# A four-layer state-space and attention kernel: side work laid out anew on the engines of its state-space layers

## The reference

```python
h = _layernorm(x, gamma, beta)
h = h * (1.0 + scale[:, None, :]) + shift[:, None, :]
h = h[:, perm]
xz = h @ W_in
xm, z = jnp.split(xz, 2, axis=-1)
xc = conv_general_dilated(xc, conv_w, ...) + conv_b      # four taps over time, per channel
xm = silu(xc)
dtr, Bm, Cm = split(xm @ W_xp, [64, 80])
dt = softplus(dtr @ W_dt + b_dt)
A = -exp(A_log)
def step(hst, inp):
    dA = exp(dt_t[:, :, None] * A)
    hst = hst * dA + (dt_t * x_t)[:, :, None] * B_t[:, None, :]
    y = einsum('bds,bs->bd', hst, C_t)
y = (y + xm * D_param) * silu(z)
return x + gate * (y @ W_out)[:, inv_perm]
```

## Time and profile before

| what | value |
|---|---|
| median of 3 runs | 2964.96 us (2961.61 to 2968.52) |
| the profiled execution | 2969.68 us, of which the span is 2968.0 us |
| TensorE busy | 2442.6 us, 82% of the span |
| VectorE | 2178.1 us, 73% |
| ScalarE | 2159.3 us, 73% |
| GpSimd | 1689.8 us, 57% |

### The profile page before, as it was taken

How to read it: one execution, slowest core, us unless ns; L and a number is a source line. 1 busy time by engine, 2 the same in 40 slices (tenths; PEclk the granted TensorE clock), 3 DMA queues, 4 the chain that set the end, 5 groups by cost and what they waited for, 6 DMA issues and landing times. The chain is left out here.

```text
span 2968.0 us, 44243 instructions
## 1 busy us (share of the span) xinstructions
PE 2442.6 (82%) x14532; PEld 1664.9 (56%) x14532; DVE 2178.1 (73%) x2878; ACT 2159.3 (73%) x3593; POOL 1689.8 (57%) x1365
## 2 busy tenths in 40 slices
PE   7778578898898898637888999857888888889885
PEld 4555257777677777512333333224576666677784
DVE  4443378888888898556777776615899988998983
ACT  3333389999999999513666656547989989999993
POOL 0000078888988989650111111004989889899895
PEclk9999799999999999867999999878999999999997
DMA  3100211112112111145555544111111112112121
GB/s 106 39 28 22 73 40 45 51 60 65 39 60 67 37 53 60 38 93 81 80 87 87 82 82 76 22 55 43 44 67 60 58 53 78 61 53 74 58 68 43
DMA packets 106124, 177.01 MB, mean 60 GB/s; under 512 B 10709, under 2 KB 91405, under 8 KB 97199
## 3 DMA queue, kind: packets, MB, share of 16 engines
q1 hardware_dynamic: 101679, 161.69, 21.3%
q0 software_dynamic: 4224, 12.59, 1.3%
HBM read 139.70 MB, written 34.14 MB: 59 GB/s over the span
## 5 line engine op out<-in xcount | busy, mean ns | idle before, releaser
L1121 POOL TENSOR_TENSOR l_h<-l_h,l_c_all 128x512 f32<-128x512 f32 x1024 | 1380.7, 1370 | 184.8 <-DVE l_h L1038 168.9
L1038 DVE TENSOR_TENSOR_SCAN l_h<-l_dA,l_ps_dbu 128x512 f32<-128x512 f32 x1024 | 1218.8, 1209 | 205.5 <-PE l_ps_dbu L1300 102.1
L1300 PE MATMUL l_ps_dbu<-ident,l_dub 128*128 128x128 f32 x4096 | 628.1, 276 | 151.0 <-DVE l_h L1038 79.7
L909 ACT ACTIVATE l_dA<-l_dt,l_a_neg 128x512 f32<-128x512 f32 x1024 | 731.1, 715 | 7.0 <-issue 5.2
L891 ACT ACTIVATE l_dub<-l_duT,l_b_tok 128x512 f32<-128x512 f32 x1024 | 730.4, 714 | 2.4 <-PE l_ps_dbu L1300 2.0
L1285 PE MATMUL l_ps_y<-ident,l_h 128*128 128x128 f32 x4096 | 623.3, 275 | 11.8 <-POOL l_h L1121 8.8
L1300 PEld LDWEIGHTS l_ps_dbu<-ident,l_dub 128*128 128x128 f32 x4096 | 471.0, 141 | 205.0 <-DVE l_h L1038 112.0
L1285 PEld LDWEIGHTS l_ps_y<-ident,l_h 128*128 128x128 f32 x4096 | 485.5, 142 | 130.8 <-issue 92.4
L1795 ACT ACTIVATE l_probs<-l_ring 128x512 f32<-128x512 f32 x512 | 292.8, 598 | 261.9 <-PE l_ring L1933 260.7
L1614 DVE TENSOR_REDUCE l_q_max<-l_ring 128x1 f32<-128x512 f32 x512 | 338.4, 683 | 175.6 <-PE l_ring L1926 171.8
L1933 PE MATMUL l_ring<-l_qs,l_ks 102*128 102x512 bf16 x512 | 201.5, 398 | 59.5 <-DMA l_qs<-l_m_parts 51.4
(11 more groups left out here) (248 smaller groups left out, 2949.7 us busy)
## 6 DMA issues: line engine op xcount, KB each, us to landing
l_c_all<-c_rows_dram SPq DMA_DIRECT2D x64, 1024.0 KB, 4.8
l_res<-x_dram SPq DMA_DIRECT2D x24, 512.0 KB, 6.0
parts_dram<-l_parts SPq DMA_DIRECT2D x48, 256.0 KB, 2.9
l_qs<-parts_dram SPq DMA_DIRECT2D x48, 256.0 KB
l_ks<-parts_dram SPq DMA_DIRECT2D x48, 256.0 KB
l_x_in<-x_dram SPq DMA_DIRECT2D x16, 512.0 KB, 7.3
x_dram<-l_res SPq DMA_DIRECT2D x16, 512.0 KB, 3.1
l_x_in<-in_x SPq DMA_DIRECT2D x8, 512.0 KB, 4.3
```

The source lines that it names most:

```text
L909: act.activation(dA[:, s % DA_RING, :], dt[:, p, j, :], ACT.Exp, scale=a_neg[:, j * N + n:j * N + n + 1]).then_inc(da_ok, 1)
L1038: dve.tensor_tensor_scan(h[:, h_slot(s), :], dA[:, s % DA_RING, :], ps_dbu[:, dbu_slot(s), :], 0.0, ALU.mult, ALU.add).then_inc(scan_ok, 1)
L1121: pool.tensor_tensor(h[:, h_slot(s), :], h[:, h_slot(s), :], c_all[:, (n // C_GROUP) % 2, n % C_GROUP, :], ALU.mult).then_inc(hc_ok, 1)
L1300: last = pe.transpose(ps_dbu[:, dbu_slot(s), t * P:(t + 1) * P], dub[:, DUB_SLOTS[n], t, j * P:(j + 1) * P], ident[:])
```

## The change

The arithmetic of the taps and of softplus is divided anew, and most step numbers move:

- **Convolution.** The last tap and the bias become an Identity pass on ScalarE that reads the projection in PSUM, in `x_part`, ahead of its copy. VectorE keeps three taps for each block, at steps 9 to 20.
- **z copies** go from ScalarE to VectorE (`z_copy`, steps 45, 47, 49, 51, the first batch excepted).
- **Softplus** drops the absolute value: VectorE writes dt and, capped at 20, a second copy (`dt_low`); ScalarE takes exp and ln of that, and the sum becomes a maximum. Sums stand at 41, 43, 45, 47, GpSimd's `dt_u` at 42, 44, 46, 48.
- **Single contractions**: `in_proj` and `out_proj` issue a half at a step (`X_AT`, `OUT_AT`).
- **Statistics** of the normalisation go from steps 25 to 27 to 31 to 33, its ScalarE parts from 31, 36, 37 to 36, 47, 48, and `mod` from 53, 55 to 54, 56.
- **Gathers** of layer 3 go from steps 4 to 12 to 18 to 24, and from 40 to 43 to 51 to 54.
- **Edge pieces.** The first batch's Silu and x projection are cut by channel block and interleaved with its z projection.
- **Layer 2.** The three DMAs of a group's maxima are issued by GpSimd right after it has made them.
- **Semaphores** are cleared by ranges.

```diff
-                for s in self.all:
-                    sp.sem_clear(s)
+                nums = sorted(s.num for s in self.all)
+                at = 0
+                while at < len(nums):
+                    end = at + 1
+                    while end < len(nums) and nums[end] == nums[end - 1] + 1:
+                        end += 1
+                    sp.sem_clear(range(nums[at], nums[end - 1] + 1))
+                    at = end
...
-PREP_V = JB * (TAPS - 1)
+X_AT = (0, 1, 3, 4, 5, 6, 7, 8)
+OUT_AT = (20, 21, 22, 23, 25, 26, 27, 28)
+PREP_V = JB * (TAPS - 2)
...
                 def x_part(b, j):
                     act.wait_ge(in_mm, b * JB + j + 1)
+                    if j == 0 and not first(b):
+                        act.wait_ge(dt_ok, b * JB)
+                    wcol = VEC_LAYOUT[L + "_conv_w"][0] + j * TAPS + TAPS - 1
+                    act.activation(work[:, j, :], bank(b, "x", j), ACT.Identity, scale=vecs[:, wcol:wcol + 1],
+                                   bias=vec(vecs, L + "_conv_b")[:, j:j + 1])
                     act.activation(conv_in[:, j, TAPS - 1:], bank(b, "x", j), ACT.Copy).then_inc(xc_ok, 1)
-                def z_part(b, p, t):
-                    act.wait_ge(z_mm, b * TB + t + 1)
-                    if t == 0:
-                        if not early(b):
-                            act.wait_ge(y_ok, b * JB - JB)
-                    act.activation(z[:, p, t, :], bank(b, "z", t), ACT.Copy).then_inc(z_ok, 1)
+                def z_first(t):
+                    act.wait_ge(z_mm, t + 1)
+                    act.activation(z[:, 0, t, :], bank(0, "z", t), ACT.Copy).then_inc(z_ok, 1)
...
+                def silu_first(j):
+                    act.wait_ge(conv_ok, j + 1)
+                    act.activation(u[:, j, :], work[:, j, :], ACT.Silu).then_inc(u_part if j < JB - 1 else u_ok, 1)
...
-                def softplus_abs(b, j):
-                    act.wait_ge(dtr_ok, b * JB + j + 1)
-                    act.activation(work[:, j, :], dt_in[:, j, :], ACT.Abs).then_inc(dti_ok, 1)
-
                 def softplus_exp(b, j):
                     act.wait_ge(dti_ok, b * JB + j + 1)
-                    act.activation(work[:, j, :], work[:, j, :], ACT.Exp, scale=-1.0).then_inc(dt_exp, 1)
+                    act.activation(work[:, j, :], work[:, j, :], ACT.Exp).then_inc(dt_exp, 1)
...
-                    if s in (3, 6, 9, 12): x_part(b, (s - 3) // 3)
-                    if s == 33: xd(b, p)
-                    if s in (40, 42, 44, 46): softplus_abs(b, (s - 40) // 2)
-                    if s in (41, 43, 45, 47): softplus_exp(b, (s - 41) // 2)
-                    if s in (42, 44, 46, 48): softplus_log(b, (s - 42) // 2)
+                    if s in (4, 7, 9, 11): x_part(b, (4, 7, 9, 11).index(s))
+                    if s == 34: xd(b, p)
+                    if s in (39, 41, 43, 45): softplus_exp(b, (s - 39) // 2)
+                    if s in (40, 42, 44, 46): softplus_log(b, (s - 40) // 2)
                     if first(b):
-                        if s in (13, 14, 15, 16): z_part(b, p, s - 13)
-                    elif s in (45, 47, 49, 51): z_part(b, p, (s - 45) // 2)
+                        if s in (13, 16, 19, 22):
+                            silu_first((s - 13) // 3)
+                            z_first((s - 13) // 3)
+                            if s == 22:
+                                act.preload_act_table_set(EXP_LN)
                     if s in (57, 59, 61, 63): du_tok(b, (s - 57) // 2)
                 def far_step(s, b):
-                    if s == 31: ln_rstd(b)
-                    if s in (36, 37): ln_apply(b, s - 36)
-                    if s in (53, 55): mod(b, (s - 53) // 2)
+                    if s == 36: ln_rstd(b)
+                    if s in (47, 48): ln_apply(b, s - 47)
+                    if s in (54, 56): mod(b, (s - 54) // 2)
...
-                        if j == 0 and not first(b):
-                            dve.wait_ge(dt_ok, b * JB)
-                        dve.tensor_scalar(work[:, j, :], conv_in[:, j, 0:T], vecs[:, wcol:wcol + 1],
-                                          vec(vecs, L + "_conv_b")[:, j:j + 1], ALU.mult, ALU.add).then_inc(prep_v, 1)
                     else:
-                        dve.wait_ge(prep_v, b * PREP_V + j * (TAPS - 1) + k)
-                        dve.scalar_tensor_tensor(work[:, j, :], conv_in[:, j, k:k + T], vecs[:, wcol + k:wcol + k + 1], work[:, j, :],
-                                                 ALU.mult, ALU.add).then_inc(prep_v if k < TAPS - 1 else conv_ok, 1)
+                        dve.wait_ge(prep_v, b * PREP_V + j * (TAPS - 2) + k)
+                    dve.scalar_tensor_tensor(work[:, j, :], conv_in[:, j, k:k + T], vecs[:, wcol + k:wcol + k + 1], work[:, j, :],
+                                             ALU.mult, ALU.add).then_inc(prep_v if k < TAPS - 2 else conv_ok, 1)
+
+                def z_copy(b, p, t):
+                    dve.wait_ge(z_mm, b * TB + t + 1)
+                    if t == 0 and not early(b):
+                        dve.wait_ge(y_ok, b * JB - JB)
+                    dve.tensor_copy(z[:, p, t, :], misc[:]).then_inc(z_ok, 1)
+                def dt_low(b, j):
+                    dve.tensor_scalar(work[:, j, :], bank(b, "dt", j), vec(vecs, L + "_dt_b")[:, j:j + 1], SOFT_TOP, ALU.add, ALU.min).then_inc(dti_ok, 1)
...
-                    dve.scalar_tensor_tensor(dt[:, p, j, :], dt_in[:, j, :], 0.0, work[:, j, :], ALU.max, ALU.add).then_inc(dt_ok, 1)
+                    dve.scalar_tensor_tensor(dt[:, p, j, :], dt_in[:, j, :], 0.0, work[:, j, :], ALU.add, ALU.max).then_inc(dt_ok, 1)
...
-                    if 9 <= s < 9 + JB * TAPS: tap(b, (s - 9) // TAPS, (s - 9) % TAPS)
-                    if s == 34: b_copy(b, p)
-                    if s in (36, 38, 40, 42): dt_raw(b, (s - 36) // 2)
-                    if s in (43, 45, 47, 49): softplus_sum(b, p, (s - 43) // 2)
+                    if 9 <= s < 9 + JB * (TAPS - 1): tap(b, (s - 9) // (TAPS - 1), (s - 9) % (TAPS - 1))
+                    if s == 35: b_copy(b, p)
+                    if s in (36, 38, 40, 42):
+                        dt_raw(b, (s - 36) // 2)
+                        dt_low(b, (s - 36) // 2)
+                    if s in (41, 43, 45, 47): softplus_sum(b, p, (s - 41) // 2)
+                    if not first(b) and s in (45, 47, 49, 51): z_copy(b, p, (s - 45) // 2)
                 def far_step(s, b):
-                    if s in (25, 26): ln_stats(b, s - 25)
-                    if s == 27: ln_moments(b)
+                    if s in (31, 32): ln_stats(b, s - 31)
+                    if s == 33: ln_moments(b)
                 def post_step(s, b, p):
-                    if s in (24, 28): out_gate(b, p, (s - 24) // 4)
+                    if s in (24, 29): out_gate(b, p, (s - 24) // 5)
...
-                            if s == 4: next_rows(b + 2)
-                            if s in (6, 8, 10, 12): gather_x(b + 2, (s - 6) // 2)
+                            if s == 18: next_rows(b + 2)
+                            if s in (21, 22, 23, 24): gather_x(b + 2, s - 21)
                         if gathered and has_post:
-                            if s in (40, 41, 42, 43): gather_y(b - 1, 1 - p, s - 40)
-                            if s in (53, 58): residual_rows(b - 1, (s - 53) // 5)
+                            if s in (51, 52, 53, 54): gather_y(b - 1, 1 - p, s - 51)
+                            if s in (59, 62): residual_rows(b - 1, (s - 59) // 3)
...
-                        if has_prep and s in (43, 45, 47, 49): dt_u(b + 1, 1 - p, (s - 43) // 2)
+                        if has_prep and s in (42, 44, 46, 48): dt_u(b + 1, 1 - p, (s - 42) // 2)
...
+                def in_proj(b, e, k):
+                    if k:
+                        pass
+                    elif e == 0:
                         pe.wait_ge(mod_ok, b * DH + DH)
                     elif not first(b):
                         pe.wait_ge(xc_ok, b * JB + e)
-                    for k in range(DH):
-                        last = pe.matmul(bank(b, "x", e), w_in[:, k, e * P:(e + 1) * P], modT[:, k, :], start=(k == 0), stop=(k == DH - 1))
-                    last.then_inc(in_mm, 1)
+                    last = pe.matmul(bank(b, "x", e), w_in[:, k, e * P:(e + 1) * P], modT[:, k, :], start=(k == 0), stop=(k == DH - 1))
+                    if k == DH - 1:
+                        last.then_inc(in_mm, 1)
                 def z_proj(b, t):
                     if first(b):
-                        pass
+                        if t == TB - 1:
+                            pe.wait_ge(z_ok, 1)
                     elif t == 0:
-                        pe.wait_ge(dtr_ok, b * JB + JB)
+                        pe.wait_ge(dti_ok, b * JB + JB)
...
+                def x_first(k):
+                    if k < JB - 1:
+                        pe.wait_ge(u_part, k + 1)
+                    else:
+                        pe.wait_ge(u_ok, 1)
```

(26 more changed lines are left out.)

52 lines of the change are left out of this document (21 added, 31 removed).

## The result

The changed kernel takes 3018.15 us (median of 4 runs, 3016.15 to 3021.37) against 2966.74 us: a ratio of 1.0177, 95% interval 1.0158 to 1.0195. The forecast was slower, by 16 us to 2981 (2925 to 3025 as range); it is slower by 51. The direction was right and the size was not, and the parts show that one of the sum's terms did not exist and that one cost was put at nothing.

A forecast was written before the change was run, and what follows sets the result against it. ScalarE nearly bounds the steady batch; TensorE's DMA waits bound the attention layer. Layer 1 +33, layer 3 +12, softplus stall +35, layer 2 -40, clears -14, openings -10 sum to +16: 2981 us, range 2925 to 3025.

The forecast's parts named there:

- wait at step 3: Batch start: TensorE waits 3.8 us for ScalarE's conv copy, done at 6.5 us; scan 9 at 20.0 us against 14.38.
- the z loop: Batch end: z projection, transposes, scan and VectorE's z copy chain at 4.75 us per two steps; ScalarE alone 3.5.
- the stall: Softplus sum at step 45, layers 1 and 3: VectorE waits on GpSimd, 2.5 us per batch, +35 in all.
- the ring of eight: First half of a batch: ScalarE's lead of up to eight units absorbs start delay; Silu ends only 1.2 us later.
- statistics that moved behind it: Normalisation statistics after the Silu, two pairs of 0.64 us on VectorE: hidden by ScalarE's table loads, no cost.
- -40 forecast: Layer 2: maxima pass the stack on GpSimd's queue, 4.1 us per wait plus some 2 of half-clock work won.
- 3.6 us that I kept as a rest: Layer 2: of TensorE's 7.7 us wait per batch, 3.6 remain because the stack lands about 1470, TensorE ready at 1466.4.
- Clears and openings: Outside the steady batches: 246 semaphore clears become a handful, -14; earlier first x projection in each layer's opening, -10.
- 1 (the stall is short): Rival, chance 0.28: VectorE waits half a GpSimd instruction, 0.64 us, at the softplus sum; 9 instead of 35, 2955 us.
- 2 (ScalarE stays the bound): Rival, chance 0.10: VectorE copies z while TensorE works on units between; batches take 105 us, kernel 2834.
- 3 (clock): Rival, chance 0.10: TensorE runs at 0.50 clock behind the batch-start wait, 2.2 us more per batch, +31, 3012 us.
- 4 (layer 2 does not do what it says): Rival, chance 0.10: maxima on the other queue still land with the stack; -40 becomes 0, kernel 3021 us.

The follow-up runs named there:

- x_start_old: The changed kernel with whole x projections and ScalarE's conv copies at their old steps, last tap still on ScalarE: 2969.74 us.
- z_and_x: The changed kernel with z copies back on ScalarE and whole x projections and conv copies at their old steps: 2904.69 us.
- gathers_40: The changed kernel with layer 3's gathers of y and row residuals back at steps 40 to 43, 53, 58: 3066.97 us.
- half_stack: The changed kernel with half the heads left out of every layer 2 stack transfer from the third batch on: 3015.47 us.
- best1: The kernel before plus range clears, layer 3's gathers at new steps and layer 2's maxima on GpSimd's queue: 2944.07 us against 2964.01.
- z_x_tap: z_and_x with the fourth tap and bias back on VectorE (16 taps, ScalarE copies only): 2964.47 us.
- z_on_act: The changed kernel with the four z copies of a steady batch back on ScalarE at the same steps: 2970.58 us.
- l2_alone: The kernel before with only layer 2's maxima issued by GpSimd, SyncE starting the stack without them: 2964.46 us against 2969.97.

## Why the prediction was wrong

- **The two loops: right in kind.** The wait at step 3 for ScalarE's copy, which is done 6.5 us into the batch as worked out, the z loop of 4.75 us per two steps (14.85 worked out, 14.9 measured) and ScalarE's 6.8 us before the modulation copy (7.05) all are in the trace, and undoing either end of the batch gives 48 us.
- **The direction was right in part by luck.** Without the stall, which does not exist, the same sum gives 2946 us: faster than before. What made the kernel slower all the same are costs of the batch that the sum had too small or not at all. The fourteen batch periods average 116.0 us where 113.0 was worked out, which is 41 us; with the edges the scans of layers 1 and 3 grew by 84 us instead of 45.
- **The start was mis-sized.** The step "the ring of eight absorbs the rest, and the Silu at step 28 ends 1.2 us later than before" failed: the Silu of u ends at 49.1 us instead of 47.1, 2.0 later. Scan 9 comes at 21.3 and not 20.0, with the clock down behind the wait, which I had put into a rival at 0.10; the wait of 3.8 us was itself 2.16. The comparison with the kernel before also hides most of what the start costs: scan 29 is at 51.1 us before, at 53.9 in the changed kernel and at 49.1 with the old start and twelve taps (x_start_old). The start costs 4.8 us, and the taps give 2.0 of them back.
- **A wait was put at nothing.** The step "the statistics that moved behind it ... are on VectorE and hidden there by ScalarE's table loads" failed, or the move of `b_copy`, which the sum doesn't have, takes its place: TensorE waits 1.85 us for that copy, and steps 29 to 36 take 1.9 us longer in the batch worked out, 24.5 us in all fourteen. So the first z copy ends at 84.9 us and not at 82.5; from there to the next batch the forecast had 31.4 us and the trace 31.6. No run tells the statistics from the copy's new step, and z_and_x still has 23.3 us of these waits.
- **The stall of +35 does not exist.** The step that took the middle between 0.09 and 4.78 for a sum with three GpSimd instructions near it failed. The largest of the four sums of a steady batch is 0.79 us, and gathers_40 shows what it takes: GpSimd behind by several instructions. I had named the backlog and then left it out. This error and the two above cancel, which is why layers 1 and 3 came out within 5 us (84 against 80).
- **Layer 2 was the costly miss**: -40 forecast, about -8 measured in the scores. Three steps of that term failed. The wait does not end with the queue order: the maxima land when the stack's traffic ends, whichever queue issues them (12 us on GpSimd's). The part won per wait was 2.3 us, not 4.1. And the clock is not won back, since 3.83 us of idle remain by ScalarE's Silu and tables, whatever the DMAs do; in half_stack the granted clock falls to 0.50 behind them too. The 3.6 us that I kept as a rest was near that number, but for another reason.
- **Clears and openings** were forecast at -24; the stretches outside scans and scores became 30 us shorter, about 6 more than forecast. In best1, which has the clears and not the new openings, they became 15.6 shorter: the clears were sized right, and the openings somewhat low.
- Of the rivals, the condition of 1 (the stall is short) came true, but not its 2955, since it kept my prices for the loops. 2 (ScalarE stays the bound) is out for this change, and z_x_tap speaks against it even for z_and_x. 3 (clock) is partly true: 1.3 us later at scan 9, and 0.7 us per batch in the mean at steps 36 to 40; its sign, a clock of 0.9 or less in layer 1, did not come (0.97). 4 (layer 2 does not do what it says) is four fifths true.
- The sum, put right on the profile: 2986, less the stall's 35, plus 39 for the batches and 32 for layer 2, less 6 for clears and openings, is 3016, the profiled execution (3016.28).

On the rule about the shared port pair, an exclusive lock for one whole instruction (the Trainium skill, SBUF - State Buffer, section SBUF: two separate sides): in the steady batches the trace agrees, no sum waits more than one instruction. In gathers_40 sums of 2.9 and 4.2 us last over more than one GpSimd instruction, as the 5.51 did; there the measurement decides, and the rule is too short. On the rule that each DMA engine takes turns between the queues, a packet at a time (the Trainium skill, DMA: Bandwidth & Descriptors, section Queues, rings and completion order): the quick passing that I had read into it is not in the trace. Issued while the DMA engines were full, a 4 KB transfer on another queue took 12 us, until they fell idle; in half_stack, issued when they were nearly idle, it took 1.6.

Why z_and_x wins more than its two parts can be read from the traces for the most part. Against the kernel before in the same runs the changed kernel is 51 us slower, z_on_act and x_start_old lie 51 and 52 below that, and z_and_x 111: 8 more than the sum, not 17. The fourteen batch periods of the profiled executions say the same (49, 55 and 112 us). The difference comes from steps 36 to 40, which vary from batch to batch with the clock: over fourteen batches they take 111.8 us in the changed kernel, 120.5 in z_on_act, 114.3 in x_start_old and 111.3 in z_and_x. Outside them the parts add up to 115 and both together win 111. What stays open is why the clock falls there in some batches and not in others.

## What to carry to other kernels

Before a wait is priced as removable, look at what each engine does under it: the next releaser (here ScalarE's Silu passes and table loads) can stand within a microsecond of the first, and then the order of queues hardly matters. Where two engines hand one bank to and fro, put the copy on the engine that runs ahead of the chain, not on the one that stands in it, even when the other is less busy. And when two new costs are estimated, check each against the trace by its place: a sum that comes out right can hide errors that cancel.

## What the hardware showed that I had not expected

- The granted clock of TensorE was low behind short waits. Behind the 2.16 us at a batch's start it is 0.57 over the next 4 us. In z_on_act, behind 1.85 us of waiting for b_tok, it is at its lower level (0.51, 1.2 GHz) for ten microseconds of full work, and steps 36 to 40 take 11.0 us instead of 7.3. TensorE's row and the stretch behind it:

```profile
892.00 1.83 PE L1260 MATMUL l_misc<-l_x_dbl,l_w_dt 64*128 64x512 f32 x2 [1.85 <-DVE l_b_tok L1010]
...
892.00:902.00 10.00, 10.00 (x33) 6.69 (x34) 6.96 (x8) 6.79 (x12) 7.52 (x7) 0.51 0.00 0
```

- It is not so in each batch: in the changed kernel steps 36 to 40 of layer 1 take 7.3 us in five of seven batches, in four of them behind waits as long. But where there is no wait for b_tok, in the kernel before, best1 and l2_alone, the granted clock of these steps is 1.00 in all fourteen batches.
- A small DMA on its own queue was no way past a stack of 3 MB on another: 12 us while the DMA engines were full, 1.6 us once the traffic was through.
- A VectorE instruction that starts just before a GpSimd instruction costs GpSimd 0.4 us (1.72 instead of 1.28) and itself 0.1; one that meets a GpSimd queue with work waiting takes VectorE 2.9 to 4.2 us instead of 0.67 (gathers_40).
